# Windowed attention with adaptive layer norm: row maxima subtracted by two more rows of the stacked queries, and the product with the values in 32-column tiles with one normalising chain per sixteen heads

## What is computed

```python
for i in range(0, S, w2):                       # S = 256, w2 = 32, w4 = 16
    start, end = max(0, i - w4), min(S, i + window_size - w4)
    attn = softmax(einsum('bqd,bkd->bqk', q[:, start:end] * scale, k[:, start:end]), axis=-1)
    wo = einsum('bqk,bkd->bqd', attn, v[:, start:end])
    ...                                         # blended with the window before: ramp 0..1 over 32 tokens
```

## Time and profile before

| | us |
|---|---|
| median of three runs (lowest, highest) | 371.27 (369.61, 377.07) |
| span of the profiled execution | 361.3 |
| time around the span, median minus span | 10.0 |
| TensorE matmuls busy | 305.9 (85%) |
| TensorE weight loads busy (beside the matmuls) | 231.7 (64%) |
| VectorE busy | 244.1 (68%) |
| ScalarE busy | 152.3 (42%) |
| GpSimd busy | 78.6 (22%) |
| mean granted TensorE clock | 0.887 of full speed |

### The profile page before, as it was taken

One profiled execution on the slowest core, in us unless ns is written; L12 is line 12 of the kernel. 1 busy time (PEld: TensorE's weight loads), 2 busy tenths in 40 slices (PEclk: granted clock), 3 DMA queues, 4 the chain that ended last, 5 costly groups with the idle time before them and its releaser, 6 DMA issues.

```text
span 361.3 us, 10050 instructions
## 1 busy us (share of the span) xinstructions
PE 305.9 (85%) x3668; PEld 231.7 (64%) x3668; DVE 244.1 (68%) x709; ACT 152.3 (42%) x298; POOL 78.6 (22%) x115
## 2 busy tenths in 40 slices
PE   2256697999898998997898979888787989989993
PEld 1123554777676876876657757556576878868892
DVE  2454605837849759488456584858887899698986
ACT  2135073337346174463551635465455313824220
POOL 4443101302304104032020011030553012202020
PEclk9766588569789699799886999999999999999998
DMA  6009386270360903505308100000000000100000
GB/s 188 24 2 201 95 175 164 79 127 4 105 98 2 185 12 98 100 6 144 60 3 181 23 5 2 2 2 2 0 2 0 2 1 0 31 0 23 8 29 29
DMA packets 38540, 20.01 MB, mean 55 GB/s; under 512 B 5604, under 2 KB 38120, under 8 KB 38504
## 3 DMA queue, kind: packets, MB, share of 16 engines
q1 hardware_dynamic: 38504, 19.53, 24.7%
HBM read 11.13 MB, written 8.13 MB: 53 GB/s over the span
## 4 chain that ended last, share of the span: by engine, by line
PE 47%; DVE 22%; issue 9%; SPq 9%; DMA 7%; ACT 4%; POOL 1%; DVEq 0%; ACTq 0%; POOLq 0%
PE bank L637 5%; PE bank L422 5%; PE bank L386 5%; PE bank L432 4%; PE bank L403 4%; DVE xh L1007 3%; PE bank L398 3%; SPq L293 3%; SPq L320 3%; DMA kst<-stack_scratch 3%; PE bank L442 3%; PE bank L619 3%; DVE acc L1342 3%; PE bank L620 2%; PE bank L621 2%
## 5 line engine op out<-in xcount | busy, mean ns | idle before, releaser
L1048 DVE TENSOR_REDUCE nm<-bank 128x8 f32<-128x512 f32 x64 | 43.3, 690 | 29.0 <-PE bank L386 28.3
L857 POOL TENSOR_TENSOR rs<-ve,mhalf 128x2 f32<-128x2 f32 (+1 forms) x24 | 19.8, 827 | 141.5 <-DVE ve L1004 134.7
L720 ACT ACTIVATE prob<-bank 128x512 f32<-128x512 f32 x64 | 37.8, 601 | 11.8 <-PE bank L403 10.0
L422 PE MATMUL bank<-prob,vb 128*64 128x128 f32 x512 | 40.7, 305 | 2.1 <-issue 1.6
L386 PE MATMUL bank<-kst,qst 48*64 48x64 bf16 x1024 | 31.0, 208 | 7.7 <-DMA kst<-stack_scratch 4.3
L809 ACT ACTIVATE sg<-bank 128x512 f32<-128x512 f32 x32 | 18.9, 600 | 43.6 <-PE bank L621 42.1
L637 PEld LDWEIGHTS bank<-wds,hh 128*128 128x128 f32 x256 | 32.3, 191 | 7.1 <-issue 5.5
L726 ACT ACTIVATE pvs<-bank 128x512 f32<-128x512 f32 x32 | 19.1, 596 | 41.9 <-PE bank L422 41.9
L386 PEld LDWEIGHTS bank<-kst,qst 48*64 48x64 bf16 x1024 | 24.4, 120 | 18.4 <-issue 18.0
L637 PE MATMUL bank<-wds,hh 128*128 128x128 f32 x256 | 33.7, 277 | 2.8 <-DVE acc L1342 2.3
L422 PEld LDWEIGHTS bank<-prob,vb 128*64 128x64 f32 x512 | 31.7, 151 | 4.4 <-issue 2.7
(11 more groups left out here) (139 smaller groups left out, 514.0 us busy)
## 6 DMA issues: line engine op xcount, KB each, us to landing
stack_scratch<-parts SPq DMA_DIRECT2D x16, 216.0 KB, 2.3
qst<-stack_scratch SPq DMA_DIRECT2D x16, 216.0 KB, 3.9
kst<-stack_scratch SPq DMA_DIRECT2D x16, 216.0 KB, 5.3
stack_scratch<-parts SPq DMA_DIRECT2D x16, 144.0 KB, 2.3
stack_scratch<-parts SPq DMA_DIRECT2D x16, 72.0 KB, 2.0
mrow<-mt SPq DMA_DIRECT2D x64, 4.0 KB, 1.7
out_x<-fin SPq DMA_DIRECT2D x4, 256.0 KB, 2.3
xs<-in_x SPq DMA_DIRECT2D x1, 896.0 KB, 6.7
```

Of the source, the lines that this page charges most:

```text
L422: m = pe.matmul(psv[WIN * (h2 % 2):WIN * (h2 % 2) + WIN, P * (h2 // 2):P * (h2 // 2) + P], vb[n][:, eo, H2 * par + h2, :, :, :], prob[gp % ...
L720: act.activation(prob[g // 2 % 2][:, :, g % 2, :], psb[g % 2][:].rearrange("p (h q) -> p h q", h=H2), ACT.Exp).then_inc(exp_done, 1)
L1048: dve.tensor_reduce(nm[:, g, :], psa[g % 2][:].rearrange("p (h k) -> p h k", h=H2), AX_X, ALU.max, negate=True).then_inc(max_done, 1)
```

## The change

1. The two bf16 parts of minus the row maxima are written as two more rows (48 and 49 of each half) of the stacked queries, where the stacked keys have ones. `scores_b` is then 16 matmuls of 50 rows, and the matmul with 512 columns, the tile `mrow` and its mask are gone. A DVE memset at the start writes the ones.
2. As the rows differ between the two window parities, there is one `qst` for each parity, of 256 columns. `read_stacks` reads 2 x 2 transfers for the queries (48 x 8 runs of 256 numbers, the second pair 32 columns further on) and 2 for the keys; `scores_a` waits for all six.
3. `probs_v` computes 16 products in place of 8, each with 32 columns of weights (one window) against the 64 moving columns of the same window, in four column tiles, so that nothing is computed in vain and sixteen heads of one parity fill one bank.
4. `copy_pv`, `turn_sums` and `normalise` are done twice a step in place of four times, for sixteen heads, and `normalise` has one product of 128 partitions in place of two of 64. The first chain comes behind A3, the second behind A7, directly ahead of the gather.

```diff
 def read_stacks(b, n):
     sp.wait_ge(b_done, after(b_done, 8 * (b - 1)))
-    for k, (stack, written) in enumerate(((qst[n], q_written), (kst[n], k_written))):
+    for k, stack, written, cols in ((0, qst[n][0], q_written, slice(0, S)),
+                                    (1, kst[n], k_written, slice(0, LINE)),
+                                    (0, qst[n][1], q_written, slice(LINE - S, LINE))):
         sp.wait_ge(written, after(written, 48 * (b + 1)))
         for r in range(2):
-            src = scr_rows[ds(b, 1), r, k].rearrange("b r h n -> (b r) h n")
+            src = scr_rows[ds(b, 1), r, k, :, :, cols].rearrange("b r h n -> (b r) h n")
             sp.dma_start(stack[64 * r:64 * r + ROWS], src).then_inc(stack_ready, 16)
 def write_mrow(b, n, hf):
     sp.wait_ge(mt_ready, after(mt_ready, 2 * b + hf + 1))
-    for part in range(2):
-        for half in range(2):
-            r = 2 * part + half
-            sp.dma_start(mrow[n][r:r + 1, 32 * hf:32 * hf + 32, :],
-                         mt[32 * part:32 * part + 32, WIN * half:WIN * half + WIN]
-                         ).then_inc(mrow_ready, 16)
+    for par in range(2):
+        for part in range(2):
+            r, at = 64 * par + ROWS + part, 32 * part + 16 * par
+            sp.dma_start(qst[n][hf][r:r + 1].rearrange("o h (s q) -> o (h s) q", s=2),
+                         mt[at:at + 16, :]).then_inc(mrow_ready, 16)
...
 def scores_a(b, n, g):
-    pe.wait_ge(stack_ready, after(stack_ready, 64 * (b + 1)))
+    pe.wait_ge(stack_ready, after(stack_ready, 96 * (b + 1)))
...
 def scores_b(b, n, g):
     bank = psb[g % 2]
-    pe.matmul(bank[:], monesb[:], mrow[n][:, H2 * g:H2 * g + H2, :], start=True, stop=False,
-              skip_group_check=True)
-    rows_ = slice(64 * par, 64 * par + ROWS)
+    rows_ = slice(64 * par, 64 * par + MROWS)
...
 def probs_v(b, n, gp):
-    for h2 in range(H2):
-        m = pe.matmul(psv[WIN * (h2 % 2):WIN * (h2 % 2) + WIN, P * (h2 // 2):P * (h2 // 2) + P],
-                      vb[n][:, eo, H2 * par + h2, :, :, :], prob[gp % 2][:, h2, :, :],
-                      start=True, stop=True)
+    if par == 0:
+        pe.wait_ge(pvs_ready, after(pvs_ready, 2 * b + eo))
+    for hg in range(2):
+        for sel in range(2):
+            for ct in range(4):
+                h2, at = 4 * hg + ct, S * par + P * hg + WIN * sel
+                m = pe.matmul(psv[32 * ct:32 * ct + 32, at:at + WIN],
+                              vb[n][:, eo, H2 * par + h2, sel, :, :], prob[par][:, h2, sel, :],
+                              start=True, stop=True)
...
 def normalise(b, eo):
-    for sel in range(2):
-        p = slice(WIN * sel, WIN * sel + WIN)
-        dst = ctxn[p, eo, :, WIN * par:WIN * par + WIN].rearrange("p f (h d) -> p f h d", d=HD)
-        ...
-        dve.tensor_tensor(dst, src, f.broadcast_to([WIN, 2, H2, HD]), ALU.mult
-                          ).then_inc(norm_step, 1)
+    dst = ctxn[:, eo, :, :].rearrange("p f (h d) -> p h f d", d=HD)
+    f = fac[:].rearrange("p h (f o) -> p h f o", o=1)
+    dve.tensor_tensor(dst, sums[:, :, :, 0:HD], f.broadcast_to([P, NH, 2, HD]), ALU.mult
+                      ).then_inc(norm_step, 1)
...
+for n in range(2):
+    for par in range(2):
+        dve.memset(kst[n][64 * par + 32:64 * par + 64].bitcast(F32), TWO_ONES).then_inc(ones_ready, 1)
```

More of the change, by code:

```diff
@@ L17 @@
+import struct
 from contextlib import ExitStack
@@ L55 @@
 ZONE_HIGH = 0.5
+TWO_ONES = struct.unpack("f", struct.pack("I", 0x3F803F80))[0]
 def build(nc, x, wqkvp, w1, w2, wg, wu, wd, wr, temp, c_t, wmod, cols, rows, ident, alpha, vmask,
-          mones, earlier, out):
+          earlier, out):
     ctx = ExitStack()
@@ L130, in build @@
         parts = sb("parts", [P, 3, 2, LINE], BF16)
-        qst = [sb(f"qst{i}", [P, H2, LINE], BF16) for i in range(2)]
-        kst = [sb(f"kst{i}", [P, H2, LINE], BF16) for i in range(2)]
         nm = sb("nm", [P, 8, H2])
@@ L900, in cut_m @@
                 apart(pool)
-                src = nm[:, 4 * hf:4 * hf + 4, :].rearrange("p g h -> p (g h)")
-                pool.tensor_copy(mp[:, 0, :], src).then_inc(mp_step, 1)
+                src = nm[:, 4 * hf:4 * hf + 4, :].rearrange("p (a s) h -> p a h s", a=2)
+                high, low = [mp[:, part, :].rearrange("p (a h s) -> p a h s", a=2, s=2) for part in range(2)]
+                pool.tensor_copy(high, src).then_inc(mp_step, 1)
                 pool.wait_ge(mp_step, after(mp_step, 4 * b + 2 * hf + 1))
-                pool.tensor_tensor(mp[:, 1, :], src, mp[:, 0, :], ALU.subtract).then_inc(mp_step, 1)
+                pool.tensor_tensor(low, src, high, ALU.subtract).then_inc(mp_step, 1)
             pool.memset(mhalf[:], -0.5).then_inc(consts_pool, 1)
@@ L1168, in step @@
                 maxima_next(1)
-                normalise(b, 0)
                 if norm:
@@ L1173, in step @@
                 maxima_next(3)
+                normalise(b, 0)
                 if group is not None:
@@ L1183, in step @@
                     cut_qk(b + 2, 1)
-                normalise(b, 1)
                 if group is not None:
@@ L1414 @@
     ramp = np.linspace(0.0, 1.0, WIN // 2, dtype=np.float32)
-    alpha = np.ones((2, WIN, 2, 2, 2), np.float32)
+    alpha = np.ones((2, WIN, 2, 2), np.float32)
     vmask = np.ones((P, 2, 2), np.float32)
```

101 lines of the change are left out of this document (46 added, 55 removed).

## The result

The changed kernel takes 388.16 us (median of 4 runs, 382.94 to 389.89); the kernel before, run beside it, takes 374.17 (369.61 to 378.56). The ratio is 1.037, 95% interval 1.023 to 1.050: slower, where "same" was forecast, and 5 us above the upper end of the range, 383.

The account below looks back on a forecast made before the run. TensorE bounds the kernel, the stack-read ring close behind and binding after the change; 2.2 (start) + 1.5 (four rings) + 0.3 (fifth) - 1.5 (end) = +2.5 us, span 363.8, plus 10.0 around it: 374 us, range 360 to 383.

Parts of the forecast that it names:

- The ring through the reads: A0 to maxima, transfers, stack reads and next A0: 20.7 us before, to become the bound with the added reads.
- the sign that was named: A0 in each full step waits for a transfer of a stack, 1 us or more.
- The reads' own price: Six stack reads a step in place of four: 2.1 us more by bytes, 2.7 by packets, 2.4 taken.
- The ring's length: A0 to next A0 in full steps: 10.4 + 10.3 + 2.4 + 0.2 = 23.3 us, 23.8 with some low clock.
- rival (b): Slower by the clock: TensorE idles, low clock over A0 to project_qk, ring 24.8 us or more; 380 us, chance 0.22.
- The slack of 3 us: Third step of the kernel before: ring of 20.7 us in a step of 23.6.
- The start: First A0 moves by 2.4 us, a maxima transfer comes 4.6 us later; 2.2 us left at A0 of 82.70.
- The end, by the clock: Steps 6 and 7, which read nothing: +0.2 for the new wait, -1.7 for fewer VectorE chains, -1.5 us in all.
- The price of the tiles: Values' product as 32 small matmuls at 23 ns: 0.74 us a group in place of 1.02, 1.1 us gained a step.
- Rival (c): Narrow tiles keep 64 ns a matmul, 2.05 us in PV1 on the path to q and k; 380 us, chance 0.06.
- VectorE and the gather: Normalise product of 128 x 256 takes 0.425 us by a like one; new wait ahead of the gather, 1.1 us per step.
- rival (a): The reads do not bind: ring 20.9 us, four rings 11.1 us less, together -14 us; 357 us, chance 0.19.

Follow-up runs that it names:

- early_last: Changed kernel with the last chain of a step moved ahead of project_v, nothing left out; 385.36 us, ratio 1.043 to the kernel before.
- one_q_early: Changed kernel with one query stack of 288 columns, four stack reads a step, and the last chain ahead of project_v; 367.73 us, ratio 0.982.
- pv_four: Kernel before with the values' product in 32-column tiles alone, its four chains a step kept; 380.40 us, ratio 1.027.
- scores_one_q: Kernel before with maxima as two more rows, the 512-column matmul gone, and one query stack, no extra reads; 365.31 us, ratio 0.976.
- each half alone: Kernel before with parts 1 and 2 of the change only, 390.55 us, ratio 1.049; with parts 3 and 4 only, 395.67 us, ratio 1.073.
- fill: Changed kernel with useless 512-column matmuls where TensorE stands, 8 ahead of A0, 5 ahead of A6, 5 ahead of the gather; 390.29 us, ratio 1.056.
- pv_alone: Kernel before with parts 3 and 4 of the change only (32-column tiles, two chains a step); 395.67 us, ratio 1.073.
- one_q_busy: one_q_early with one useless matmul of 128 rows and 512 columns ahead of each B group; 375.16 us, ratio 1.020 to the kernel before.
- one_q_fill: one_q_early with 4 useless matmuls of 128 rows and 512 columns ahead of A0 and 4 ahead of A6; 377.18 us, ratio 1.024.

## Why the prediction was wrong

**What bounds the kernel: right in the main.** The ring through the reads became a bound of the steps: A0 waits for a stack in six of its eight places, and taking the two reads away again is worth 18.6 us of the span in the form of early_last. But the sign that was named, 1 us or more in each full step, came in two of six; a path at the low clock through q and k to VectorE and A6 runs beside the ring and is about as long.

**The reads' own price: right.** 2.4 us a step were taken. Where A0 waits, parts to A0 is 13.6 and 13.7 us (166.91 less 153.34, the parts of that step; 192.89 less 179.22) with six reads and 11.3 with four: 2.3.

**The ring's length: wrong, and this is one of the two failed steps.** It was put at 10.4 + 10.3 + 2.4 + 0.2, with 0.5 added for the clock: 23.8. It measures 25.1 to 26.0. Two of its terms were too small. The 10.3 us for parts to A0 were read off the quiet of the DMA queues at 127.2, in a step in which A0 did not wait; where it waits, the same transfers take 11.3 in one_q_early. In the kernel before itself they took 12.6 at the one full step in which A0 waited, from

```profile
163.76 4.25 SPq L275 DMA_DIRECT2D stack_scratch<-parts  x6
```

to the A0 at 176.36. And A0 to parts, taken as 10.4 because "VectorE sets it at full clock", is 11.5 to 12.7: A0 to project_qk runs at the low clock, the copy of the turned maxima in the step from 116.22 starts at

```profile
125.73 0.21 DVE L1059 COPY mt<-bank 64x128 bf16<-64x128 bf16 x1
```

9.5 us behind A0, and stood 7.3 behind it before. The second is rival (b)'s mechanism, the first nobody's, and (b)'s ring of 24.8 was still short. The slack of 3 us that the prediction saw in a step would by 11.3 be 23.6 less (10.4 + 11.3), 1.9.

**The start: sized wrong.** The first A0 stands at 38.62, forecast 39.6. But 2.2 us were left for all behind it, and 4.0 had come in by the gather of step 0. The maxima's transfer, said to come 4.6 us later, is waited for there, 2.59 us where it was 0.86:

```profile
68.57 1.06 PE L407 MATMUL bank<-qst,kst 50*64 50x64 bf16 x32 [2.59 <-DMA qst<-mt]
```

A stall of 2.29 us in the middle of B3 of the second step, which counts in the five steps, was foreseen by nobody:

```profile
89.72 0.37 PE L407 MATMUL bank<-qst,kst 50*64 50x64 bf16 x5 [2.29 <-issue]
```

The profile names no releaser for it. It was not tested.

**The end, by the clock: wrong in sign, the other failed step.** "In step 7 two chains fewer on VectorE, -1.7" and +0.2 for the gather: -1.5 in all. Measured +7.4, of which 4.8 is TensorE busy for longer and 2.5 standing (0.9 at A0), and another +2.4 behind the last gather, where the mean clock is 0.96 for 0.99. The prediction took the full clock of the earlier trace rows for given; the clock was 0.52. It treated the clock as something lost by waits alone, three of about a microsecond, and so asked only over which few groups it would be low. That the clock would be low for 133 us more than in the profile before, because products of 32 columns by 64 stand where products of 64 by 128 stood, was in none of the cases. So of the 30 us by which the matmuls' busy time was to fall, 1.8 came. Rival (b) had the sign and most of the path, at 0.22, and its end "gives nothing" where the end lost 10.

**The price of the tiles: right at full clock.** 0.74 us a group, taken from the B groups; a group and the start of the next one, first at full clock, then at the low one:

```profile
113.34 0.65 PE L430 MATMUL bank<-prob,vb 128*32 128x64 f32 x32
113.93 0.44 PE L407 MATMUL bank<-qst,kst 50*64 50x64 bf16 x16
...
118.40 1.08 PE L430 MATMUL bank<-prob,vb 128*32 128x64 f32 x32
119.41 1.33 PE L360 MATMUL bank<-x1t,wa 128*128 128x288 f32 x2
```

0.59 us at full clock, less than taken, 18 ns a matmul. At the low clock it is 1.01, as much as the old group's 1.02 at full clock: the whole saving is gone. Rival (c) falls.

**VectorE and the gather: right.** The product of 128 x 256 takes 0.42 us, as estimated from its like, and the gather waits 1.13 to 1.22 us where 1.1 was forecast. The end of the fourth full step shows the path, the last maximum and the three operations behind it:

```profile
158.06 0.69 DVE L1053 TENSOR_REDUCE nm<-bank 128x8 f32<-128x512 f32 x1 [2.68 <-PE bank L391]
159.18 0.36 DVE L1067 RECIPROCAL rsum<-bank 128x32 f32<-128x32 f32 x1 [0.43 <-PE bank L440]
159.57 0.19 DVE L1069 TENSOR_TENSOR fac<-rsum,alph 128x32 f32<-128x32 f32 x1
159.80 0.42 DVE L1075 TENSOR_TENSOR ctxn<-bank,fac 128x256 f32<-128x256 f32 x1
```

early_last, which takes this wait away, gains nothing by the ratio: the ring takes it back.

**Sums.** From 82.70 to 176.36 are 93.7 us, as the sum has it, but that is 23.4 a step and not 23.7; for rival (a) it makes 10.1 less and not 11.1, so 358. The 10.0 us "around the span" are not around it: in the executions whose time and span are both known these lie 1.7 to 3.5 us apart, and the rest is the difference between the profiled execution and the median. The forecast of 374 was in effect the median plus 2.5, where 14.0 were measured.

**What stays open.** The clock was lost by the values' half: pv_four, with the narrow tiles alone, executed at 0.72 to 0.77 beside a kernel before at 0.84 to 0.87 and lost 2.7%, while scores_one_q, without the 512-column matmuls, kept the clock of the kernel before beside it and gained 2.4%. What the low clock costs in time, apart from the reads, is not known: each half alone costs more than both, and fill gave the clock back without a gain. What the merged chains add (pv_alone at 0.71) is open too, and so is why executions of one kernel differ in their clock.

## What to carry to other kernels

Work taken off TensorE pays only at the clock at which the rest runs: here small tiles brought the granted clock down and cost more than the products in vain that they replaced, so price a removal at both clocks, and look at the granted clock of the half-changed kernel first. Where a second engine or queue is a few microseconds behind the bound, measure its ring in a step where something waits for it, and keep new transfers out of it: the same rows in one stack, written a little later, made the kernel 2% faster than before where two stacks had made it 4% slower.

## What the runs showed of the hardware

- 128 more matmuls of 512 columns: on 128 rows the clock was 1.00 and two steps took 46.6 us; on 4 rows 0.55 and 67.1 us, at 95% busy.
- In three executions of the kernel before, in one batch, the mean clock and the span moved together: 363.8 us at 0.869, 370.6 at 0.849, 377.0 at 0.824, some 3 us per 0.01.
- In seven kernels with a larger hardware loop TensorE stalled for 2.1 to 6.0 us at the jump back, and the instruction queue fetched nine or ten packets more; 16 matmuls more in one_q_early's loop did not bring this (one_q_busy, 26 packets), 16 and four waits did (one_q_fill, 35).
